# The first slot's rows picked on TensorE, and POOL's queue of weight splits rewritten, in a mixture-of-experts kernel

## What is computed

```python
c = x @ W.T + scal[a] * ((x @ A[a].T) @ Bm[a].T)      # a: the adapter of the batch row
w = softmax_integer(c @ w_gate.T)                     # fixed-point softmax over 8 experts
top_w, top_i = top_k(w, 2); top_w = top_w / top_w.sum()
for e in range(8):
    h = silu(c @ w1[e].T) * (c @ w3[e].T)             # 704 hidden features
    out = out + combine[:, e:e + 1] * (h @ w2[e].T)
x = x + out
```

## Time and profile before

| | us |
|---|---|
| median of 3 runs | 231.97 (231.13 to 232.19) |
| the profiled execution | 231.47 |
| its span, first to last instruction | 229.4 |
| PE busy | 205.3 (89%) |
| POOL busy | 150.7 (66%) |
| DVE busy | 100.7 (44%) |
| ACT busy | 85.5 (37%) |
| mean granted clock of PE | 0.97 of full |

### The profile page before, as it was taken

The page is one execution under the profiler, slowest core; times in us unless marked ns, Lnnn a source line. Parts: engine busy times, 40 slices in busy tenths (PEclk is TensorE's granted clock), DMA queues, the critical chain, the costliest instruction groups (busy, mean ns, idle before and its releaser), DMA issues.

```text
span 229.4 us, 3961 instructions
## 1 busy us (share of the span) xinstructions
PE 205.3 (89%) x1227; PEld 176.8 (77%) x1227; DVE 100.7 (44%) x297; ACT 85.5 (37%) x232; POOL 150.7 (66%) x131
## 2 busy tenths in 40 slices
PE   7699995999999999999993799099999999999993
PEld 5479973888888888888982688088887988888891
DVE  0758886353343534344332135013533444336814
ACT  2656760599423333232331123012322323226610
POOL 8100066969969998998999799989984453188000
PEclk9999998899999999999999799859999999999999
DMA  6994317999345104064505540440051111019004
GB/s 158 414 372 160 123 60 223 379 372 331 118 161 176 37 24 139 24 206 130 171 18 188 181 139 16 169 140 23 1 186 69 70 49 69 23 47 322 22 3 183
DMA packets 16146, 32.66 MB, mean 142 GB/s; under 512 B 2080, under 2 KB 10400, under 8 KB 16000
## 3 DMA queue, kind: packets, MB, share of 16 engines
q1 hardware_dynamic: 12304, 25.17, 33.0%
q0 software_dynamic: 2160, 5.64, 7.0%
q10 hardware_dynamic: 1664, 1.61, 2.2%
HBM read 25.59 MB, written 6.82 MB: 141 GB/s over the span
## 4 chain that ended last, share of the span: by engine, by line
POOL 37%; PE 32%; DMA 14%; issue 10%; ACT 3%; POOLq 1%; DVE 1%; SPq 0%; DVEq 0%; ACTq 0%
POOL w_all L423 18%; PE gu L1095 9%; DMA rows<-cond_rows,src_i 8%; POOL rows L417 7%; POOL w_all L490 6%; PE gu L1102 4%; DMA expert_rows<-rows,dst_i 3%; DMA x<-x_t 3%; PE gu L981 3%; PE ya L1132 2%; POOL w_all L436 2%; POOL expert_rows L448 2%; PE ht L1109 2%; PE ya L1133 2%; PE ya L1134 2%
## 5 line engine op out<-in xcount | busy, mean ns | idle before, releaser
L1095 PE MATMUL gu<-w_all,xs_hi 128*128 (+2 forms) x276 | 75.2, 396 | 13.5 <-POOL w_all L436 11.8
L1095 PEld LDWEIGHTS gu<-w_all,xs_hi 128*128 128x128 f32 x276 | 48.6, 195 | 22.2 <-issue 17.5
L835 DVE TENSOR_TENSOR hid<-gu,sg 128x256 f32<-128x256 f32 x46 | 19.5, 425 | 91.9 <-ACT sg L593 88.8
L593 ACT ACTIVATE sg<-gu 128x256 f32<-128x256 f32 x46 | 17.7, 385 | 93.9 <-PE gu L1102 91.8
L423 POOL TENSOR_TENSOR w_all<-raw,w_all 128x1024 fp32r<-128x1024 f32 (+2 forms) x15 | 46.8, 3123 | 1.1
L1102 PE MATMUL gu<-w_all,xs_lo 128*128 (+1 forms) x138 | 42.1, 387 | 2.6 <-DVE xs_lo L827 2.6
L417 POOL DMA_INDIRECT rows<-cond_rows,src_i x23 | 23.1, 1005 | 30.0 <-DMA cond_rows<-c_rows 23.7
L1132 PE MATMUL ya<-w_all,h_hi 128*128 (+1 forms) x115 | 38.7, 337 | 0.0
L448 POOL DMA_INDIRECT expert_rows<-rows,dst_i x20 | 19.7, 987 | 21.1 <-DVE hid L835 8.7
L1133 PE MATMUL ya<-w_all,h_hi 128*128 (+1 forms) x115 | 32.9, 286 | 0.0
L1134 PE MATMUL ya<-w_all,h_lo 128*128 (+1 forms) x115 | 32.5, 282 | 0.0
(11 more groups left out here) (193 smaller groups left out, 280.1 us busy)
## 6 DMA issues: line engine op xcount, KB each, us to landing
raw<-expert_weights SPq DMA_DIRECT2D x6, 896.0 KB, 4.8
raw<-expert_weights SPq DMA_DIRECT2D x6, 640.0 KB
raw<-expert_weights SPq DMA_DIRECT2D x6, 512.0 KB
expert_rows<-zeros SPq DMA_DIRECT2D x1, 2048.0 KB
rows<-expert_rows SPq DMA_DIRECT2D x8, 256.0 KB, 4.7
cond_rows<-c_rows ACTq DMA_DIRECT2D x4, 256.0 KB, 2.1
raw<-x_t SPq DMA_DIRECT2D x1, 1024.0 KB
out_t<-raw SPq DMA_DIRECT2D x4, 256.0 KB, 2.2
```

Source lines behind the costliest of these rows:

```text
L1095: nc.tensor.matmul(out, stay_hi[:, kc * P:(kc + 1) * P], moving(at, part + first + kc * P, n), start=kc == 0 and part == HI_COLS, stop=False)
```

## The change

- The first slot's rows are no longer gathered. DVE makes a one-hot `picks` from the positions of expert 0's tokens (`first_pos`, `row_no`), and PE multiplies `c_rows` with it, 16 products of 128 columns in plain float32, straight into `xt`. They stand ahead of the row-number products, which now go to another PSUM bank. The first batch of gathers is slots 1 to 3. SP's load of expert 2 also waits for these products.
- The ranks' products stand earlier among the conditioned rows; the 16 warming products are gone.
- ACT copies expert 0's first piece before `g_both`, DVE subtracts it in two halves in the router's chain; the second piece and `slot_lo(0)` go ahead of the row numbers' copy; the third piece and the tail follow the destinations.
- Tails are split in place: the third copy takes the tail's 256 columns along (`HI_PIECES`), and the tail subtraction overwrites the lower 64 rows of the stack with raw minus stack. `tail_hi`, `low_done`, `w_split0` and `raw_free[2]` go; SP's third load waits for `w_ready`.
- `tail_low` waits for no landing; for experts 4 to 7 the copy of the next piece stands ahead of a piece's subtraction.
- One scatter moves from expert 5's round to expert 7's; the weights of the choices are worked out in four parts in items 54 to 57; the shares are fetched behind scatter 15.

```diff
-KEEP_WARM = 16
-GATHERED = [(0, 4), (4, 6), ...]
-SCATTERED = {4: (0, 2), 5: (2, 5), 6: (5, 6), 7: (6, 7)}
+HI_PIECES = [PIECES[0], PIECES[1], slice(DOWN_AT, HI_COLS)]
+GATHERED = [(1, 4), (4, 6), ...]
+SCATTERED = {4: (0, 2), 5: (2, 4), 6: (4, 5), 7: (5, 7)}
+SHARES_AT = ITEMS - 15
+SHARES_BEHIND = 15
...
     raw_weights(e):
-                    if turn_of(e):
+                    if turn_of(e) and k < 2:
                         sp.wait_ge(raw_free[k], turn_of(e))
+                    elif turn_of(e):
+                        sp.wait_ge(w_ready, in_raw_before(e) + 1)
...
+            sp.wait_ge(xt_done, 1)
             sp.wait_ge(rows_in[1], 16)
             raw_weights(2)
...
             def tail_low(e):
-                recent = gathered_beside(e - 1, 2) if e > 1 else range(*GATHERED[0])
-                for s in [*recent, *gathered_beside(e, 0), *gathered_beside(e, 1)]:
-                    pool.wait_ge(rows_in[s], 16)
-                if e in SCATTERED:
-                    pool.wait_ge(scattered, ...)
-                return nc.gpsimd.tensor_tensor(stack_part(e, 1), raw_tail(e, LOWER), as_f32(tail_hi[e % 2][LOWER, :]),
-                                               ALU.subtract)
+                stack = stack_part(e, LOW_HALF)
+                return nc.gpsimd.tensor_tensor(stack, raw_tail(e, LOW_HALF), as_f32(stack), ALU.subtract)
...
-                pool.wait_ge(low_done, e)
-                pool.wait_ge(whi_ready, 4 * e + 4)
-                pool.wait_ge(w_ready, e)
                 tail_low(e).then_inc(w_ready, 1)
-                pool.wait_ge(w_ready, e + 1)
-                if from_raw(e) is raw:
-                    pool.sem_inc(raw_free[2], 1)
+                if e == STAGED:
+                    pool.wait_ge(w_ready, e + 1)
                 beside_piece(e, 2)
...
-                for k, cols in enumerate(PIECES):
+                high(0)
+                for k in range(len(PIECES)):
+                    if k < 2:
+                        high(k + 1)
                     steps += 1
-                    pool.wait_ge(raw_in[k], RAW_LOADS[k] * (turn_of(e) + 1))
-                    nc.gpsimd.tensor_copy(hi_part(e, cols), raw[:, cols]).then_inc(whi_step, 1)
                     pool.wait_ge(whi_step, steps)
                     ins = low(e, k)
...
-                nc.gpsimd.tensor_copy(tail_hi[e % 2][:, :], raw_tail(e)).then_inc(whi_step, 1)
-                nc.gpsimd.tensor_copy(stack_part(e, 0), raw_tail(e, slice(0, TAIL))).then_inc(whi_step, 1)
-                pool.wait_ge(whi_step, steps)
                 tail_low(e).then_inc(w_ready, 1)
-                pool.wait_ge(w_ready, e + 1)
-                pool.sem_inc(raw_free[2], 1)
                 beside_piece(e, 2)
...
     ACT
+            expert_hi(0, 0)
             act.wait_ge(g_done, 1)
...
-            expert_hi(0, 0)
             expert_hi(0, 1)
             c_copy(0)
             c_copy(1)
             expert_hi(0, 2)
-            expert_tail_hi(0)
+            expert_hi(1, 0)
             c_copy(2)
             c_copy(3)
...
     DVE
             mask_part(1)
+            first_lo(0)
             xa_lo_part(1)
             pk_lo_part(slice(PK_W, PK_G), 2)
+            first_lo(1).then_inc(raw_free[0], 1)
...
+            beside(nc.vector.scalar_tensor_tensor(first_pos[:, :], by_tile(full(other))[:, :, 0], 1.0,
+                                                  picked[:, 0:TILES, 0], ALU.add, ALU.mult))
...
+            nc.vector.tensor_tensor(picks, row_no[:, :].unsqueeze(1).broadcast_to([P, TILES, P]),
+                                    first_pos[:, :].unsqueeze(2).broadcast_to([P, TILES, P]),
+                                    ALU.is_equal).then_inc(picks_ready, 1)
...
+            expert_lo(1).then_inc(raw_free[1], 1)
+            slot_lo(0)
             dve.wait_ge(src_done, 1)
...
             destinations()
-            weights_of_choices()
-            expert_lo(0, 2)
-            expert_tail_lo(0)
-            slot_lo(0)
+            expert_lo(2)
+            expert_tail_lo().then_inc(w_ready, 1)
...
     PE
             conditioned(0)
-            conditioned(1)
+            base(2)
...
             last.then_inc(ranks_done, 1)
+            base(3)
+            low_rank(2)
+            low_rank(3).then_inc(c_done, 1)
             conditioned(2)
             conditioned(3)
+            pe.wait_ge(picks_ready, 1)
+            for kc in range(KC):
+                for t in range(TILES):
+                    pe.wait_ge(c_out, t // 2 + 1)
+                    last = nc.tensor.matmul(xt[:, kc * P:(kc + 1) * P], c_rows[:, t, kc * P:(kc + 1) * P],
+                                            picks[:, t, :], start=t == 0, stop=t == TILES - 1)
+            last.then_inc(xt_done, 1)
...
-            pe.wait_ge(c_out, TILES // 2)
-            for _ in range(KEEP_WARM):
-                nc.tensor.matmul(gu[GU_BANKS - 1][:, :], zeros[:, :], wide_zeros, start=True, stop=True)
```

More of the change, by code:

```diff
@@ L166, in moe_kernel @@
         h_lo = [sb(f"h_lo{i}", [P, 2 * P], F32R) for i in range(HBUFS)]
-        tail_hi = [sb(f"tail_hi{i}", [P, DIM], F32R) for i in range(2)]
+        raw_low_tail = sb("raw_low_tail", [P, DIM])
         raw = sb("raw", [P, HI_COLS])
@@ L259, in moe_kernel @@
         raw_low_in = [sem(f"raw_low_in{k}") for k in range(len(PIECES))]
[L260 to L261 removed]
+        raw_free = [sem(f"raw_free{k}") for k in range(len(PIECES) - 1)]
         w_ready = sem("w_ready")
@@ L367, in _ @@
                 raw_weights(e)
-            for k in range(len(PIECES)):
-                sp.wait_ge(raw_free[k], EXPERTS - 2)
+            sp.wait_ge(w_ready, EXPERTS)
             sp.dma_start(x_back, x_dram[:, :, :]).then_inc(x_back_in, 16)
@@ L507, in _ @@
                            allow_small_or_imprecise_dtypes=True).then_inc(pool_step, 1)
-            pool.wait_ge(share_at_ready, 1)
-            pool.wait_ge(share_out, 16)
-            for l in range(DIRECT):
-                nc.gpsimd.indirect_dma_start(
-                    out=share[:, l:l + 1], out_offset=None, in_=share_dram[:, :],
-                    in_offset=bass.IndirectOffsetOnAxis(ap=share_at[:, 2, l:l + 1], axis=0)).then_inc(share_in, 16)
             for s in range(SCATTERED[EXPERTS - 1][1], SENT):
@@ L517, in _ @@
                 scatter(s)
+                if s == SHARES_BEHIND:
+                    pool.wait_ge(share_at_ready, 1)
+                    pool.wait_ge(share_out, 16)
+                    for l in range(DIRECT):
+                        nc.gpsimd.indirect_dma_start(
+                            out=share[:, l:l + 1], out_offset=None, in_=share_dram[:, :],
+                            in_offset=bass.IndirectOffsetOnAxis(ap=share_at[:, 2, l:l + 1],
+                                                                axis=0)).then_inc(share_in, 16)
             pool.wait_ge(pool_step, 4)
@@ L579, in _ @@
             expert_hi(0, 2)
-            expert_tail_hi(0)
+            expert_hi(1, 0)
             c_copy(2)
             c_copy(3)
-            for k in range(len(PIECES)):
-                expert_hi(1, k)
-            expert_tail_hi(1)
+            expert_hi(1, 1)
+            expert_hi(1, 2)
             def silu(i):
@@ L687, in xa_lo_part, with first_lo @@
                                         ALU.subtract).then_inc(xa_lo_ready, 1)
+            def first_lo(half):
+                cols = slice(half * ITEM_COLS, (half + 1) * ITEM_COLS)
+                dve.wait_ge(whi_ready, 1)
+                return nc.vector.tensor_tensor(lo_part(0, cols), raw[:, cols], as_f32(hi_part(0, cols)), ALU.subtract)
             pk_lo_part(slice(0, PK_W), 1)
@@ L890, in _, with weights_of_choices @@
-            for k in range(2):
-                expert_lo(0, k).then_inc(w_split0, 1)
-                dve.wait_ge(w_split0, k + 1)
-                dve.sem_inc(raw_free[k], 1)
+            def weights_of_choices(part):
+                by_choice = weight[:, :].rearrange("p (k t) -> p k t", t=TILES)
+                if part == 0:
+                    chain(nc.vector.tensor_scalar(rs[:, total, :], rs[:, total, :], 1.0, None, ALU.max))
+                    beside(nc.vector.reciprocal(rs[:, most, :], rs[:, total, :]))
+                    chain(nc.vector.tensor_tensor(masked[:, :, :], mask[:, :, :],
+                                                  full(poly).unsqueeze(1).broadcast_to([P, TOP, TILES * EXPERTS]),
+                                                  ALU.mult))
+                if part == 1:
+                    chain(nc.vector.tensor_reduce(weight[:, :],
+                                                  masked[:, :, :].rearrange("p k (t e) -> p (k t) e", e=EXPERTS),
+                                                  AX_X, ALU.add))
+                    chain(nc.vector.tensor_tensor(by_choice, by_choice,
+                                                  rs[:, most, :].unsqueeze(1).broadcast_to([P, TOP, TILES]),
+                                                  ALU.mult))
+                if part == 2:
```

(6 more changed lines are left out.)

131 lines of the change are left out of this document (54 added, 77 removed).

## The result

The changed kernel takes **220.6 us** (median of 4 runs, 220.41 to 220.81) against 231.69 (231.13 to 232.19): a ratio of 0.9522, 95% interval 0.9496 to 0.9549. The profiled execution took 220.67, its span is 218.3. Of those six executions one, the profiled one, counts as slow (225.34, more than 1.5% above the fastest), but the other five take 221.93 to 224.91 as well.

A forecast was written before the change was run, and what follows sets the result against it. The end was set by when POOL announces expert 7, plus seven slots and a fixed tail. Along POOL's queue 0.3 - 3.3 - 1.9 - 4.0 - 0.3 = -9.2 us, so 231.47 - 9.2 = 222.3 us, range 220 to 225.5.

The forecast's parts named there:

- The frame: The end is when POOL announces expert 7, plus seven slots and a fixed tail; PE's earlier gains are lost at stops.
- The start: Router to POOL's first subtraction: picks 3.7 us, expert 0 announced at 37.7, POOL starting 0.3 us later, at 37.8.
- the wrong rule: GpSimd can't write descriptors while DVE holds the shared ports; a gather beside the third piece costs 0.5 us more.
- Rival 1: PE runs the 16 picks products at half clock, so 3.7 us becomes 7.4 ahead of POOL's start: 226.0 us, chance 0.15.
- Rival 2: POOL's landing waits only move, as gathers can't be queued deeper; 3.3 us comes back: 225.6 us, chance 0.10.
- Rival 3: Third weight pieces land late and hold up POOL's copies; waits sum to 13.1 us: 235.4 us, slower, chance 0.04.
- Experts 4 to 7: POOL's queue: fewer small copies and a wider third, -0.57 us each; reordered copies, -0.42 each; together -4.0 over four experts.
- term (b): POOL's queue: three gathers behind a tail start after 0.15 us, as those behind a piece do; -1.9 us.
- the stretch from slot 16 to the end as long as before (63.0 us): Sign on PE: slot 16 to the end stays 63.0 us; the prediction is wrong if longer by more than 1.5.
- The tail: End of kernel: later choices' weights, share gathers and scatters cost nothing; with the slower store up to 1.5 us.

The follow-up runs named there:

- e3: Changed kernel with the first slot gathered again: no picks, the 16 warming products back; 222.12 us.
- e5: Changed kernel with POOL's waits for gathers and scatters ahead of the tail subtractions back; 228.96 us.
- e7: Changed kernel with the five gathers of slots 18 to 22 moved behind expert 7's announcement; 221.22 us.
- e4: Changed kernel with 8 warming products back on PE ahead of slot 0; 224.49 us.
- e1: Changed kernel with PE's wait for the next expert back at the slot's first product; 224.37 us.
- e2: Kernel before with only PE's wait for the next expert moved one item ahead, to the down products; 231.04 us.
- e9: Changed kernel unaltered, run again as control beside e10 and e11; 223.87 us.
- e10: Changed kernel with the shares' weights made early and their three gathers ahead of the scatters, as in the kernel before; 220.95 us.
- e11: e10 with gathers 18 to 22 also moved behind expert 7's announcement; 220.90 us.
- e12: e11 with POOL's late gathers and share gathers spread between the scatters, planned as at most two indirect DMAs in a row; 214.75 us.
- e6: Changed kernel with each piece's copy directly ahead of its subtraction for experts 4 to 7; 226.47 us.
- e8: Changed kernel with the first slot gathered as in e3 and the five gathers late as in e7; 220.39 us.

## Why the prediction was right, and where it wasn't

**The frame held.** Time is the announcement of expert 7 plus a fixed rest. e3, e5 and e7 moved the announcement by -1.3, +6.2 and -5.6 against the changed kernel's, and slot 16's start by -1.3, +6.2 and -5.6: one for one. e4, which moved only PE, changed nothing that reached slot 16.

**The start** came out at 37.82 (forecast 37.8), term by term: picks at 3.7, row numbers at 33.06 (33.4), tail of expert 0 ended at 37.31 (37.7). One of the gathers was the later end, 37.79. It took 1.69 us beside DVE's third piece of 1.48 us, where the gather ahead of it, beside DVE's small steps, took 0.95; so the piece cost it 0.74. The prediction named the wrong rule for this. The Trainium skill, "SBUF — State Buffer", SBUF: two separate sides, keeps GpSimd from writing descriptors while DVE runs an instruction in a 2-port mode. Further on, under Who interferes with whom, the section gives `tensor_tensor`, DVE's operation here, no such mode. It says there instead that a DVE instruction with two inputs in SBUF contends with a GpSimd instruction that reads SBUF. This subtraction has two such inputs and the gather reads its row numbers there, so the trace fits that; no run here tells the two mechanisms apart.

**Rival 1**, half clock in the products, fell at once: 0.23 each is the full clock's price, in spite of 1.47 us of idle time ahead of them, and the granted clock was 1.00 from 28 to 32. It fell at 34.5, until 41.4, where e4 shows the half clock to be free. One reading behind this rival was wrong: the kernel before was not at full rate everywhere else, its granted clock was also half from 147.6 to 154.5, with the stop of 6.18 us. The Trainium skill, "FP8 and Floating Point Precision", TensorE Precision Notes, counts four passes for true FP32, which makes 128 columns cost as much as 512 in one pass; the trace agrees, 0.23 us against the 0.23 of the earlier trace rows.

**Rival 2**, landing waits that only move: no row of the changed profile waits for a landing of rows, and e5 shows that they are real waits of 4.6 us.

**Rival 3**, third pieces that come late, is there in small: 0.64 us for expert 7 and nothing for experts 5 and 6; the loads of 640 and 896 KB took 4.1 and 5.2 us at the median, not 12.7. The forecast had set this at nothing for 7.2 us of cover. The load was issued at 139.35 and the scatter ahead of the copy ended at 145.44, so the cover was 6.1 us, and the copy got its data at 146.08, 6.7 behind the issue.

**Experts 4 to 7.** -0.99 a piece for copies and gaps fits the intervals between tails of experts 4 (-1.11), 5 (-1.57, with 0.63 for its gather) and 6 (-2.97, with the scatter's 1.30). For expert 7 the terms give +0.31, with the scatter's 1.30, and -0.12 was measured. Two errors cancel in part: the 0.64 above, and a wait in the kernel before that term (b) didn't name. It counted the gathers behind a tail; behind expert 6's tail stood a copy, and it waited as well (POOL's timeline of the kernel before):

```profile
149.82 1.04 POOL L490 CAST w_all<-raw 128x1024 fp32r<-128x1024 f32 x1 [0.95 <-POOLq L485]
```

**The step that failed** is "the stretch from slot 16 to the end as long as before (63.0 us)". It took 60.95. The hunk that moves PE's wait for `w_ready` from a slot's first product to the down products ahead of it is not in the prediction's sum at all and so stood at nothing; it takes 0.2 to 0.3 us off every slot, and only the six waits behind slot 16's first product count. e1 and e2 show it in both kernels; in e2 it is 1.44 of the 2.05 us. Of the 0.6 left, 0.5 is slot 17, which in the kernel before follows the gathers of shares; that was not tried by itself. The 1.6 us by which the profiled execution came out below the forecast are these 2.05 and 0.5 on experts 4 to 7, less the 0.6 ahead of slot 16 and the 0.3 outside the span. The kernel before even had a row of it, the 0.16 of "issue" ahead of slot 21 in the earlier trace rows.

**The tail** was set at nothing, with up to 1.5 for a slow store. In the first profile that is so: the store landed in 1.4 us, the gathers of shares ran from 184.42, and the last scatter started at 192.07. But the series that the move brings about is what the stall goes with, and the kernel run again took 3.3 us more. The prediction asked only when the last of those DMAs would end; it didn't ask what seven at a stretch do to the other engines.

**What stays open.** That the stall goes with a dense series of indirect DMAs on POOL is shown by e9, e10 and e11, which ran on one chip: with the series gone from 190 us it is gone there, and with a new series at 150 it comes there. That spreading them removes it is seen in e12 alone, without a control on its chip. How the stall comes about is not shown: ACT and DVE start some 2 us after the products that they need have ended, and the profile names no releaser for it ("remote"). Nor is it known why the first four runs of the changed kernel went without it, with the same seven DMAs from 184.42 to 193.0. A series alone, in a kernel without the rest, was not tried.

## What to carry to other kernels

When the chain goes through a queue written out by hand, sum the change along that queue from its first step to the last announcement, and read each moved wait of the consuming engine too: here a wait ahead of a slot's first product cost every slot 0.2 to 0.3 us although it was long met. Work that one engine no longer has to do in time (here five gathers) is worth most when it is taken out from ahead of the last announcement, but spread it: the same indirect DMAs nearly in a row took 6 us more than with pauses (e11 against e12, on different chips). Run an unaltered control beside late experiments; without e9 the 3 us of e1, e4 and e6 would have been ascribed to their edits, and e12, which had none, proves less for it.

## What was not expected of the hardware

- Behind five or more indirect DMAs of POOL, one every 1.25 to 1.3 us, ACT's gate started 1.8 to 2.5 us after PE's turning had ended, in e9 and seven of the variants, and 0.9 us after it in e11, where at most 0.3 is usual; not in every execution (220.4 to 220.8 against 221.9 to 225.3 us for one and the same kernel).
- A wait of PE on a semaphore that is long met, ahead of a slot's first product, costs 0.2 to 0.3 us a slot (7.12 in e1 against 6.84, mean of four slots from slot 16 on).
- A gather of 128 rows took 0.95 us, beside one of DVE's long subtractions 1.69, in e3, e7, e8 and e9 1.88 to 2.02.
- PE's granted clock was full (2.4 GHz) through the picks in spite of 1.47 us of idle time ahead of them, and half (1.2 GHz) from 34.5 to 41.4.
